# A one-core Flamingo-style block: value products together with a quad of score estimates between the next sequence's score pairs, with the fourth quad and a norm moved

## The reference, cut to what matters

```python
x = x + jnp.tanh(g_xattn[0]) * _L0_xattn_ref(_layernorm(x), ctx_768, Wq, bq, ...)   # cross attention to the context
x = x + jnp.tanh(g_ffn[0]) * _L0_ffn_ref(_layernorm(x), ...)

# _L0_ffn_ref: causal self attention, then a mixture of four experts, each token with its best two
h = _rms(x, n1_w); q = _rms(heads(wq), qn_w); k = _rms(heads(wk), kn_w); v = heads(wv)
scores = where(causal, q @ k.T * HD ** -0.5, -inf); x = x + softmax(scores) @ v @ wo.T
xf = _rms(x, n2_w); probs = softmax(xf @ gate_w.T); topv, topi = top_k(probs, 2)
o0 = gelu(xf @ e0_up.T) @ e0_down.T
o1 = silu(xf @ e1_w1.T) * (xf @ e1_w2.T) @ e1_down.T
o2 = gelu(gelu(gelu(xf @ e2_l1.T) @ e2_l2.T) @ e2_l3.T) @ e2_l4.T
o3 = gelu(gelu(xf @ e3_down.T) @ e3_up.T) @ e3_out.T
return x + wts[:, 0:1] * o0 + wts[:, 1:2] * o1 + wts[:, 2:3] * o2 + wts[:, 3:4] * o3
```

## Time and profile before

| | |
|---|---|
| median of 3 runs | 1189.64 us (1189.31 to 1192.32) |
| the profiled execution, its own time | 1192.36 us |
| its span | 1190.6 us |
| TensorE (PE) busy | 1038.0 us, 87% |
| VectorE (DVE) busy | 792.6 us, 67% |
| ScalarE (ACT) busy | 735.7 us, 62% |
| GpSimd (POOL) busy | 351.5 us, 30% |
| mean granted TensorE clock | 0.941 of 2.4 GHz |

### The profile page before, as it was taken

One profiled execution on the slowest core, in us unless ns is written; L12 is line 12 of the kernel. 1 busy time (PEld: TensorE's weight loads), 2 busy tenths in 40 slices (PEclk: granted clock), 3 DMA queues, 4 the chain that ended last, 5 costly groups with the idle time before them and its releaser, 6 DMA issues.

```text
span 1190.6 us, 26283 instructions
## 1 busy us (share of the span) xinstructions
PE 1038.0 (87%) x8578; PEld 645.1 (54%) x8578; DVE 792.6 (67%) x2153; ACT 735.7 (62%) x1329; POOL 351.5 (30%) x522
## 2 busy tenths in 40 slices
PE   3647798999999998999999999999999898988797
PEld 1324455555555565555565665555565555555454
DVE  7266666767777767777767676767767676764523
ACT  1334566767576666767666766767666676756353
POOL 4611415133141414133141514224141513214030
PEclk8667789999999999999999999999999999999899
DMA  5144444433434444333344444334344443220300
GB/s 179 32 119 107 120 108 120 110 101 90 103 67 115 119 116 119 90 99 99 93 88 115 119 116 106 90 100 98 79 114 115 119 114 98 82 45 34 83 1 18
DMA packets 78693, 114.27 MB, mean 96 GB/s; under 512 B 9153, under 2 KB 41537, under 8 KB 78529
## 3 DMA queue, kind: packets, MB, share of 16 engines
q1 hardware_dynamic: 78368, 111.58, 37.2%
...
## 4 chain that ended last, share of the span: by engine, by line
PE 55%; issue 17%; DVE 15%; ACT 6%; POOL 3%; DMA 2%; SPq 2%; DVEq 0%; POOLq 0%; ACTq 0%
PE ps_w L1157 11%; PE ps_pv L1131 7%; PE ps_s2a L1110 7%; PE ps_s2b L1110 5%; DVE mpadB L888 4%; PE ps_w L1175 4%; PE ps_t L1016 3%; PE ps_w L1016 3%; PE ps_w L1060 3%; DMA qdB<-mTB 2%; SPq L528 2%; PE ps_w L1092 2%; ACT probs L766 2%; DVE mpadA L888 2%; PE ps_w L1030 2%
## 5 line engine op out<-in xcount | busy, mean ns | idle before, releaser
L766 ACT ACTIVATE probs<-ps_s2a 120x512 f32<-120x512 f32 (+1 forms) x256 | 152.9, 597 | 129.7 <-PE ps_s2a L1110 124.6
L888 DVE TENSOR_REDUCE mpadA<-ps_w 128x4 f32<-128x480 f32 x256 | 150.3, 652 | 50.6 <-PE ps_w L1092 50.6
L888 DVE TENSOR_REDUCE mpadB<-ps_w 128x4 f32<-128x512 f32 x256 | 158.8, 685 | 28.9 <-PE ps_w L1092 28.9
L1157 PE MATMUL ps_w<-W,hid 128*128 128x96 f32 x1024 | 142.4, 298 | 18.6 <-DVE split_q L797 16.0
L1157 PEld LDWEIGHTS ps_w<-W,hid 128*128 128x128 f32 x1024 | 134.9, 212 | 33.8 <-DVE split_q L797 20.8
L766 ACT ACTIVATE probs<-ps_s2b 120x512 f32<-120x512 f32 (+1 forms) x256 | 152.6, 596 | 0.2 <-PE ps_s2b L1110 0.2
L666 POOL TENSOR_SCALAR_AFFINE_SELECT probs<-probs 128x1024 f32<-128x1024 f32 x128 | 140.0, 1093 | 0.0
L630 POOL TENSOR_TENSOR rB<-veB,neg_half 128x4 f32<-128x4 f32 x16 | 16.1, 1008 | 394.4 <-DVE veB L790 394.4
L1110 PE MATMUL ps_s2a<-qdB,kstB 128*128 128x512 f32 x128 | 66.1, 517 | 38.9 <-DMA qdB<-mTB 32.5
L1175 PE MATMUL ps_w<-xfT,W 128*128 128x512 f32 x160 | 85.0, 620 | 0.0
L665 POOL TENSOR_TENSOR tick<-one 128x1 f32<-128x1 f32 x128 | 24.9, 195 | 186.9 <-ACT probs L766 183.1
...
## 6 DMA issues: line engine op xcount, KB each, us to landing
...
```

The costliest lines, as they stand in the source:

```text
L766: nc.scalar.activation(probs[0:k, slot_of(part, *index), :], bank[0:k, :], ACT.Exp, scale=SCALE if part == "A" else 1.0).then_inc(done, 1)
L888: nc.vector.tensor_reduce(mneg[OP[part]][:, :, c, b], bank[:, 0:HT * k].rearrange("p (h k) -> p h k", h=HT), AX.X, ALU.max, negate=True).t ...
L1157: ins = mm(bank[:, b * UP:(b + 1) * UP], hid[:, HID_AT[h] + k, b * P:(b + 1) * P], w[f"down{index[1]}"][:, k * UP:(k + 1) * UP], start=k = ...
```

## The change

Entries of the list move. In the self and the cross attention, the value products of a sequence now stand next to an estimate quad, between the two score pairs of the next sequence or between pair and pair; the fourth quad of B and its `mT` move from the end of the step to the end of the cross attention and to just before `e2_l1`; the norm of part N moves ahead of `wo` 1; D's squares move behind `qT` and `kT`; and `A norm`, `gates` and `v` of B and N shift by a place. In two places VectorE makes the block-diagonal keys before the low part instead of after it. The third group's step gets the same moves, and the step with the parts B, D and M (step 16) gets a list of its own.

```diff
 def self_attention():
-            + exact("D", 1, 0) + estimate("A", 0) + exact("D", 1, 2)
-            + one("B", "squares", 0, None) + values("D", 0)
-            + exact("D", 2, 0) + estimate("A", 1) + exact("D", 2, 2)
-            + values("D", 1) + one("B", "sums", 0, None) + down(0)
-            + exact("D", 3, 0) + one("D", "oT", 0, "t") + estimate("A", 2) + exact("D", 3, 2)
-            + values("D", 2) + one("D", "nT", 0, "t") + one("B", "root", 0, None))
+            + exact("D", 1, 0) + estimate("A", 0) + values("D", 0) + exact("D", 1, 2)
+            + one("B", "squares", 0, None) + estimate("A", 1) + one("B", "sums", 0, None)
+            + exact("D", 2, 0) + values("D", 1) + exact("D", 2, 2) + down(0)
+            + exact("D", 3, 0) + one("D", "oT", 0, "t") + estimate("A", 2) + values("D", 2) + exact("D", 3, 2)
+            + one("D", "nT", 0, "t") + one("B", "root", 0, None))
 def second_experts():
-            + one("D", "nT", 1, "t") + one("A", "mT") + fill("M", "e2_l3", 0) + one("D", "wo", 1, "t")
-            + one("D", "out", 0, None) + one("D", "squares", 0, None) + one("N", "norm", 0, None) + one("B", "qT") + one("B", "kT")
+            + one("D", "nT", 1, "t") + one("A", "mT") + fill("M", "e2_l3", 0) + one("N", "norm", 0, None) + one("D", "wo", 1, "t")
+            + one("D", "out", 0, None) + one("B", "qT") + one("B", "kT") + one("D", "squares", 0, None)
 def cross_attention():
-    return (one("B", "v") + exact("A", 0, 0) + down(2) + exact("A", 0, 2) + one("N", "xT")
-            + exact("A", 1, 0) + estimate("B", 0) + exact("A", 1, 2)
-            + one("D", "norm", 0, None) + one("B", "init", 0, None) + one("B", "copy", 0, None) + values("A", 0)
-            + exact("A", 2, 0) + estimate("B", 1) + exact("A", 2, 2)
-            + values("A", 1) + down(3) + one("M", "store", 0, None) + one("D", "xfT")
-            + exact("A", 3, 0) + one("A", "oT", 0, "t") + estimate("B", 2) + exact("A", 3, 2)
-            + values("A", 2) + one("D", "logits") + one("A", "nT", 0, "t"))
+    return (exact("A", 0, 0) + one("B", "v") + down(2) + exact("A", 0, 2) + one("N", "xT")
+            + exact("A", 1, 0) + estimate("B", 0) + values("A", 0) + exact("A", 1, 2)
+            + one("D", "norm", 0, None) + one("B", "init", 0, None) + one("B", "copy", 0, None) + estimate("B", 1)
+            + exact("A", 2, 0) + values("A", 1) + exact("A", 2, 2) + down(3) + one("M", "store", 0, None) + one("D", "xfT")
+            + exact("A", 3, 0) + one("A", "oT", 0, "t") + estimate("B", 2) + values("A", 2) + exact("A", 3, 2)
+            + estimate("B", 3) + one("D", "logits") + one("A", "nT", 0, "t"))
 def first_experts():
-            + one("D", "gates", 0, None) + fill("D", "e1_w1", 1, "w") + one("A", "oT", 1, "t") + fill("D", "e1_w2", 1, "w")
-            + one("A", "nT", 1, "t") + fill("D", "e2_l1", 0) + one("A", "wo", 1, "t") + one("A", "stats", 0, None)
-            + one("N", "base", 0, None) + estimate("B", 3) + fill("D", "e2_l1", 1) + fill("D", "e3_down", 0) + one("N", "q")
-            + one("D", "gates", 1, None) + one("A", "norm", 0, None) + one("N", "v") + one("B", "mT") + one("N", "k")
+            + fill("D", "e1_w1", 1, "w") + one("A", "oT", 1, "t") + one("D", "gates", 0, None) + fill("D", "e1_w2", 1, "w")
+            + one("A", "nT", 1, "t") + one("B", "mT") + fill("D", "e2_l1", 0) + one("A", "wo", 1, "t") + one("A", "stats", 0, None)
+            + one("N", "base", 0, None) + fill("D", "e2_l1", 1) + fill("D", "e3_down", 0) + one("N", "q")
+            + one("D", "gates", 1, None) + one("N", "v") + one("A", "norm", 0, None) + one("N", "k")
...
+def last_self_keys():
+    return (of_parts("BDM", self_attention())
+            + fill("M", "e2_l2", 0) + one("D", "wo", 0, "t") + one("B", "scale", 0, None) + fill("M", "e2_l2", 1)
+            + values("D", 3) + fill("M", "e3_up", 0) + one("D", "oT", 1, "t") + one("B", "qT") + one("B", "kT")
+            + fill("M", "e3_up", 1) + one("D", "nT", 1, "t") + fill("M", "e2_l3", 0) + one("D", "wo", 1, "t")
+            + one("D", "out", 0, None) + one("D", "squares", 0, None) + estimate("B", 0) + fill("M", "e2_l3", 1, "w")
+            + one("B", "v") + down(2) + estimate("B", 1)
+            + one("D", "norm", 0, None) + one("B", "init", 0, None) + one("B", "copy", 0, None)
+            + down(3) + one("M", "store", 0, None) + estimate("B", 2) + one("D", "xfT") + one("D", "logits")
+            + fill("D", "e1_w1", 0, "w") + fill("D", "e1_w2", 0, "w") + estimate("B", 3)
...
-TAIL = [(NG - 1, "ABDM", of_parts("ABDM")), (NG, "BDM", of_parts("BDM")), (NG + 1, "DM", last_self_values()), (NG + 2, "M", last_experts())]
+TAIL = [(NG - 1, "ABDM", of_parts("ABDM")), (NG, "BDM", last_self_keys()), (NG + 1, "DM", last_self_values()), (NG + 2, "M", last_experts())]
...
                     elif (part, work) in (("N", "q"), ("N", "k")):
+                        if work == "k":
+                            block_diagonal_keys(part, "A", g)
                         low_part(st, "N", "A", work, ALU.add, col["b" + work])
                         if work == "k":
-                            block_diagonal_keys(part, "A", g)
```

20 lines of the change are left out of this document (12 added, 8 removed).

## The result

The changed kernel takes 1232.7 us (median of 4 runs, 1231.6 to 1233.6) against 1189.5 us before: a ratio of 1.036, 95% interval 1.034 to 1.038. It is slower by 43 us. I had forecast 1187, and the time lies outside my range of 1171 to 1203.

What follows compares the result with a forecast made beforehand. PE, busy 87% of the span, bounds the kernel by its work plus its waits. Loop +4.8 us and -7 outside give -2, so 1190 us for the profiled execution and 1187 for the median; range 1171 to 1203.

Steps and rivals of the forecast that it cites:

- steps 1 to 4: Loop passes without a dip: new waits replace the DMA wait, 66.36 us becomes 67.5, twelve passes take 810.0 us.
- step 5: Clock in the loop: four dips in 12 passes instead of ten, 6.1 us, bounds 0 and 24.
- step 6: Outside the loop: step 16 -5 us, step 15 -1, steps 1 and 2 -1, together -7, bounds -3 and -13.
- (a): Slower rival: clock dips stay in every pass, 1199 us with one a pass, 1217 with two; chance 0.22.
- Step 3: Fourth quad: waits 1.1 us, then 0.8 before the logits; `e3_down` 2.15 us late, N's `q` 1.8 late.
- Step 4: `hT`: waits 1.5 us for VectorE's `split_k` instead of 2.22 for the DMA, 1.15 us later in the pass.
- Steps 1 and 2: Attention quads: self attention +0.2 us, with 0.8 waiting at its second quad; cross attention's `split_q` wait ends, `down(3)` 0.3 earlier.
- (b): Much faster rival: VectorE's chain is shorter, `hT` doesn't wait, passes 66.0 us, 1163 us, half of it 1176; chance 0.20.
- (c): Rival: `mTB` still lands last because the fourth quad's reductions end late, leaving 1189 us; chance 0.05.
- (d): Rival: the attentions' first quads cost more than set down, 1.0 us in each of 12 passes, 1199 us; chance 0.08.

Runs made afterwards that it cites:

- experiment 3: Kernel before with only the fourth quad and `mT` moved early: 1201.3 to 1201.7 us in three runs, 1219.9 to 1223.9 in three others.
- experiment 12: experiment 7 with step 16 in plain order, gates 1 and 2 ahead of N's `q`, low part first: 1153.4 us, ratio 0.970.
- experiment 5: Changed kernel with step 16 run over the step's list without N and A instead of its own: 1230.1 us, ratio 1.033.
- experiment 4: Kernel before with only the new list of the third group's step: 1187.5 us, ratio 0.996.
- experiment 1: Changed kernel with the low part again ahead of the block-diagonal keys on VectorE: 1227.3 us, ratio 1.029.
- experiment 7: Changed kernel with the gate logits and `nT` 0 ahead of the fourth quad and A's last value products behind it: 1180.0 us, ratio 0.991.
- experiment 13: Changed kernel with gates 1 and 2 ahead of N's `q` and the low part first: 1211.4 us, ratio 1.017.
- experiment 2: Changed kernel with the fourth quad and `mT` back in their old places: 1179.6 us, ratio 0.990.
- experiment 6: experiment 2 with the fourth quad one expert product and one `wo` earlier, `mT` ahead of N's `q`, low part first: 1203.4 us, ratio 1.011.
- experiment 8: Kernel before with only the value products, `v` and N's norm moved as in the change: 1175.1 us, ratio 0.987.
- experiment 11: Changed kernel with gates 1 and A's norm ahead of N's `q`, gates 2 ahead of `k`, low part first: 1244.1 us, ratio 1.044.
- experiment 14: experiment 12 with `base` of N ahead of A's `stats`: 1153.0 us, ratio 0.967.

## Why the prediction was wrong, and where it was right

| step | predicted us | measured us |
|---|---|---|
| the 12 passes of the loop without their dips, against 66.36 (steps 1 to 4) | 12 * 1.15 = +13.7 | 12 * 1.7 = +20 |
| dips in the loop (step 5), 1.5 to 1.6 us each | 4 instead of 10 | 21 instead of 10 |
| steps 1 and 2 outside the loop (step 6) | -1 | -4.7 |
| step 15 (step 6) | -1 | +2.0 |
| step 16 (step 6) | -5 | +6.4 |

**Step 5 failed, and is the largest part.** I took four dips of the clock because each new wait was shorter than the one of 2.22 us that had brought them. There were 21: 17 * 1.5 = 26 of the 43 us between my -2 and the +41.3 of the profiled execution. The length of a single wait was the wrong measure: 16 of the 21 stand behind two waits close together, of 1.20 and 0.85 us, each shorter than the 1.29 us that I had seen without a dip. My rival (a) had the mechanism, one or two dips a pass, at a chance of 0.22, and priced two a pass at 1217 us. What no step of mine could have said is which: experiment 3 shows passes with equal waits at 1.00 and at 0.95. The rule of the Trainium skill that I weighed there (TensorE: Matmul & The Clock Gate, A second HAM failure mode: psum-queue depth-cycling: short idle times between groups that go round PSUM banks can make the clock go up and down) fits the changed kernel, and I was wrong to set it aside on one pass. It isn't the whole: in experiment 12 PE still waits 0.7 to 1.0 us at three places of every pass, and the clock is 1.00 in all twelve.

**Step 6 failed in sign.** For step 16 I took the wait for `mTB` and half of the waits between the quads as won. The wait for `mTB` at its end is still 1.62 us (2.38 before), and I never looked for the new waits: the first quad's reductions stand behind D's squares on VectorE (3.37 us), and the clock there is 0.85, against 0.92 before. Undoing the list (experiment 5) gives 4.2 us of the step back. 2 us of it stay, and in the changed kernel `hT` of step 16 waits 1.78 us for `hb`, which it didn't before. Step 1 gained 10.0 us where I had the loop's trade, about 1; half went back in step 2, and in experiment 4 two fifths. For step 15 I wrote that without N there is no `split_k` before `hT`. But its `hT` waits 2.06 us for the `split_k` of step 14's N, and its quad and logits wait 1.12 and 0.85 us. No run tries the step by itself; with the low part first it takes 66.2 instead of 68.1 us (experiment 1), with the quad covered 64.4 (experiment 7), with both and the short chain 61.8 (experiment 12).

**Step 3 was right, and it is the loss by cause.** I had 1.1 and 0.8 us, the chip 1.20 and 0.85. `e3_down` and N's `q`, set down as 2.15 and 1.8 us late, come 2.5 and 2.2 us late, counted from the third quad in the kernel before and in a pass of experiment 13 at the full clock. Experiments 2 and 7 show that this place is the loss, and 13 against 12 its price, waits and dips together: 47 us in a loop. I took the waits as small because they stood beside a wait of 2.2 us that would go.

**Step 4 had the chain, too short.** 2.04 us for 1.5: the gate product beside `xb` took 0.99 us, and 0.39 in the kernel before. What I didn't see is what it meant: VectorE's chain was next in line behind the DMA. In experiments 3, 6 and 7 the wait of 2.22 us for the DMA is gone or nearly so, and 1.11 + 0.91, 1.94 and 2.05 us of waits for `split_k` and `ym` stand in its place. That an early `mT` alone would be worth nothing in the kernel before is argued from these: in each of them the quad or its neighbours moved as well.

**Steps 1 and 2 erred on the careful side.** The second quads wait 0.7 and 1.0 us for their banks in the changed kernel; I had 0.8 for the first and set down nothing for the second. The wait of `down(2)` for `split_q` went. Together with the norm they give 0.75 us a pass (experiment 8), where I had 0.1, and fewer dips.

Of the rivals, (b) described a kernel that is to be had (experiment 12), by a condition the change doesn't meet; (c) is out, since `mTB` lands in time, and (d), since its place gains 0.75 us a pass. Two of my sums were off without bearing on this: (a) decides from 1194.6, not 1194.8, and (c) at 1189 leaves out step 16's 5 us.

That the dips behind the logits come with the quad's place is shown: the changed kernel and experiments 1, 3, 11 and 13 have them there, experiments 2, 7, 12 and 14 have none there. That the two waits bring a dip each time isn't: six passes in a row in experiment 3 and one in 13 have both waits and a clock of 1.00. Why experiment 3 changed from one kind of pass to the other stays open.
